# A two-layer attention and expert kernel: the second layer's gate weights are turned on VectorE instead of TensorE

## What is computed

```python
logits = jnp.dot(x, Wr) + br                                  # 32 per token
aff = jax.nn.sigmoid(logits)
top_v, top_i = jax.lax.top_k(aff, 8)
top_w = top_v / (jnp.sum(top_v, axis=-1, keepdims=True) + 1e-09)
w_full = zeros((T, 32)).at[arange(T)[:, None], top_i].set(top_w)
shared = dot(silu(dot(x, Wg_s) + bg_s) * (dot(x, Wu_s) + bu_s), Wd_s) + bd_s
gate = silu(einsum('th,ehi->eti', x, Wg) + bg)
up = einsum('th,ehi->eti', x, Wu) + bu
down = einsum('eti,eih->eth', gate * up, Wd) + bd
routed = einsum('te,eth->th', w_full, down)
```

## Time and profile before

| | |
|---|---|
| three runs | 491.8, 491.97 and 492.65 us, median 491.97 |
| profiled execution | 493.67 us |
| its span, first to last instruction | 491.9 us |
| instructions | 8510 |
| mean granted TensorE clock | 0.99 of full |
| TensorE / VectorE / ScalarE / GpSimd busy | 455.2 / 398.6 / 281.6 / 269.6 us |
| the 16 transposes of `weights1` on TensorE, one | 273 ns |
| the 4 copies to `hs` on ScalarE, one | 585 ns |
| store of 64 KB to `wt_dram`, issue to landing | 1.6 us median, 3.4 us at most |

### The profile page before, as it was taken

The page is one execution under the profiler, slowest core; times in us unless marked ns, Lnnn a source line. Parts: engine busy times, 40 slices in busy tenths (PEclk is TensorE's granted clock), DMA queues, the critical chain, the costliest instruction groups (busy, mean ns, idle before and its releaser), DMA issues.

```text
span 491.9 us, 8510 instructions
## 1 busy us (share of the span) xinstructions
PE 455.2 (93%) x3072; PEld 219.5 (45%) x3072; DVE 398.6 (81%) x812; ACT 281.6 (57%) x456; POOL 269.6 (55%) x237
## 2 busy tenths in 40 slices
PE   2999888889999999999999999999889998989995
PEld 2755447434444345453454444544334453423332
DVE  1634457999998988899999978978999999986785
ACT  2264673446767635738876445556776537467640
POOL 6322360235554775547763459636675865546982
PEclk9999997999999999999999999999999999999998
DMA  7900059786952710232569643025592662204201
GB/s 277 338 14 0 22 182 194 127 142 182 234 111 76 127 18 4 73 84 65 176 181 168 111 62 91 1 65 171 178 172 43 121 98 77 58 5 113 59 2 43
DMA packets 54754, 52.44 MB, mean 107 GB/s; under 512 B 5080, under 2 KB 44344, under 8 KB 54072
## 3 DMA queue, kind: packets, MB, share of 16 engines
q1 hardware_dynamic: 54712, 51.90, 44.2%
HBM read 37.47 MB, written 13.89 MB: 104 GB/s over the span
## 4 chain that ended last, share of the span: by engine, by line
PE 73%; DVE 18%; ACT 3%; issue 2%; POOLq 1%; DMA 1%; POOL 1%; SPq 0%; DVEq 0%; ACTq 0%
PE bank L785 10%; PE bank L776 9%; PE bank L797 8%; PE scores L816 8%; PE bank L871 5%; DVE nmax L1335 3%; PE scores L711 3%; PE scores L702 3%; PE scores L726 3%; PE scores L705 3%; PE scores L810 3%; PE scores L750 3%; DVE h L1311 3%; PE bank L876 2%; DVE h L1318 2%
## 5 line engine op out<-in xcount | busy, mean ns | idle before, releaser
L1136 POOL TENSOR_TENSOR gb<-gb,wb 128x512 f32<-128x512 f32 x64 | 84.3, 1318 | 94.3 <-ACT gb L1024 76.3
L1039 ACT ACTIVATE pk<-scores 128x1024 f32<-128x1024 f32 x96 | 95.3, 1023 | 38.9 <-PE scores L816 38.7
L1129 POOL TENSOR_SCALAR_AFFINE_SELECT pk<-pk 128x512 f32<-128x512 f32 (+1 forms) x96 | 82.1, 864 | 39.8 <-ACT pk L1039 39.3
L1335 DVE TENSOR_REDUCE nmax<-scores 128x8 f32<-128x1024 f32 x64 | 76.4, 1216 | 7.7 <-PE scores L816 7.0
L1021 ACT ACTIVATE gt<-bank,bgh 128x512 f32<-128x512 f32 (+1 forms) x68 | 46.7, 687 | 62.5 <-PE bank L776 50.7
L785 PE MATMUL bank<-xnt,wu 128*128 128x512 f32 x128 | 68.3, 615 | 2.3 <-DVE h L1318 2.2
L776 PE MATMUL bank<-xnt,wg 128*128 128x512 f32 x128 | 69.4, 624 | 0.0
L797 PE MATMUL bank<-h,wd 128*128 128x512 f32 x128 | 66.5, 617 | 0.0
L1311 DVE SCALAR_TENSOR_TENSOR h<-gt,gb 128x512 f32<-128x512 f32 x64 | 57.8, 903 | 3.4 <-PE bank L797 3.1
L1318 DVE SCALAR_TENSOR_TENSOR h<-bank,bu,h 128x512 f32<-128x512 f32 x64 | 48.1, 751 | 10.8 <-PE bank L785 8.8
L1140 POOL TENSOR_TENSOR orms<-oms,minus_half 128x32 f32<-128x32 f32 x8 | 44.7, 5585 | 10.3 <-DVE oms L1365 10.3
(11 more groups left out here) (262 smaller groups left out, 711.1 us busy)
## 6 DMA issues: line engine op xcount, KB each, us to landing
wb<-wt_scratch SPq DMA_DIRECT2D x64, 256.0 KB, 4.2
parts_scratch<-parts SPq DMA_DIRECT2D x16, 384.0 KB, 3.0
qa<-parts_scratch SPq DMA_DIRECT2D x32, 192.0 KB, 4.9
ka<-parts_scratch SPq DMA_DIRECT2D x32, 192.0 KB, 5.9
parts_scratch<-parts SPq DMA_DIRECT2D x16, 256.0 KB, 3.1
parts_scratch<-parts SPq DMA_DIRECT2D x16, 128.0 KB, 2.8
ha<-in_wkq SPq DMA_DIRECT2D x1, 1024.0 KB, 4.8
wb<-in_wvo SPq DMA_DIRECT2D x1, 1024.0 KB, 7.5
```

Of the source, the lines that this page charges most:

```text
L1039: A(dst.rearrange("p (h m) q -> p m h q", m=2), pairs[pair_of(step)][:, :, :].rearrange("p m (h q) -> p m h q", q=cols), ACT.Exp, scale=SC ...
L1129: pool.affine_select(out=dst, in_=dst, compare_op=ALU.is_ge, fill=0.0, base=0, pattern=[[0, heads], [1, P]], channel_multiplier=-1).then_i ...
L1136: pw(gb[:, c % 2, :], gb[:, c % 2, :], wb[:, k % 2, j % 2, :], ALU.mult).then_inc(s_ga_done, 1)
L1335: V.tensor_reduce(dst, src, AX, ALU.max, negate=True).then_inc(s_nmax_done, 1)
```

## The change

The four transposes and the copy of `weights1` are gone from TensorE and ScalarE, and `weights1` from the orders `FRONT` and `BANK4`. Instead `choose1` ends on VectorE with one more instruction: a transpose of `wtok`, taken as 128 x 128, into the new `wturn`. VectorE's transpose works in blocks of 32 by 32, so `wturn` holds, in partition 32 g + e and column 32 k + j, the weight of expert e for token 128 k + 32 g + j. Before it stands a wait for the store of the chunk before. The step `weights1` of SyncE now waits for `s_w_done` and stores `wturn` to the same place in `wt_dram`, with an address pattern that puts each run of 32 tokens where it belongs. The 32 rows of `hs` for the shared expert are loaded back from `wt_dram` by SyncE in the step `wb/8c`, before the two transfers of `wb`; for chunks 2 and 3 this first waits until `down` of the chunk two before is done. `down` of the shared expert waits for that load, `s_wt_in`.

```diff
--- before.py
+++ after.py
@@ -69,11 +69,10 @@
 
 
 FRONT = ("load", "norm0", "scale0", "turn0", "keys0", "router0", "inner0", "scores0", "picks0", "probs0", "hidden0",
-         "hidden1", "out0", "back0", "norm1", "scale1", "turn1", "router1", "choose1", "queries1", "keys1", "store", "values1",
-         "weights1")
+         "hidden1", "out0", "back0", "norm1", "scale1", "turn1", "router1", "choose1", "queries1", "keys1", "store", "values1")
 RING = ("turn0", "keys0", "inner0", "scores0", "picks0", "probs0", "hidden0", "hidden1", "out0", "turn1", "router1",
         "queries1", "keys1", "values1", "max", "score", "fin")
-BANK4 = ("minus", "values", "weights1", "out1")
+BANK4 = ("minus", "values", "out1")
 
 
 def order(text):
@@ -239,6 +238,7 @@
         rest1 = sb("rest1", [P, TILES, E1])
         wsum = sb("wsum", [P, TILES])
         wtok = sb("wtok", [P, TILES, E1])
+        wturn = sb("wturn", [P, TILES * E1])
         hs = sb("hs", [INNER + E1, 2, CHUNK])
         wb = sb("wb", [P, 2, 2, CHUNK])
         qkf = sb("qkf", [P, 4, CHUNK])
@@ -365,8 +365,7 @@
         s_rl_done = sem("rl_done")
         s_rexp_done = sem("rexp_done")
         s_w_done = sem("w_done")
-        s_wt_ps = sem("wt_ps")
-        s_wt_sb = sem("wt_sb")
+        s_wt_in = sem("wt_in")
         s_wt_stored = sem("wt_stored")
         s_wb_in0 = sem("wb_in0")
         s_wb_in1 = sem("wb_in1")
@@ -423,7 +422,7 @@
                    s0_ps=CB, nb0=1, p0_done=TILES, pt_ps=CB, pt_sb=CB, att_ps=1, logits_ps=1, u_ps=1, lsub=1,
                    lexp_done=1, um_done=2, umt_ps=2, umt_sb=2, inter_ps=FB, inter2_ps=FB, ha_done=FB, hb_done=FB,
                    hsum_done=FB, zt_ps=1, zt_sb=1, z_ps=1, z_read=1, th0_done=TILES, var1=1, rstd1=1, xn1_done=TILES, xnt1_ps=1,
-                   xnt1_sb=1, router_ps=1, rl_done=1, rexp_done=1, w_done=1, wt_ps=1, wt_sb=1, wt_stored=16,
+                   xnt1_sb=1, router_ps=1, rl_done=1, rexp_done=1, w_done=1, wt_in=16, wt_stored=16,
                    qk_ps=4, qk_rest=4, part1=4, part2=4, part3=4, parts_stored=16 * 6, v_ps=2, v_sb=2,
                    max_ps=CB * UNITS, nmax_done=CB * UNITS, mp_done=CB, mrow_ps=CB, mrow_sb=CB, mrow_in=CB * MROWS_IN,
                    sc_ps=CB * UNITS, pk_done=CB * UNITS, pk_masked=CB * UNITS, pv_ps=CB * GROUPS, 
@@ -507,8 +506,6 @@
                 pe.wait_ge(s_mrow_sb, at(c, "mrow_sb", rest[0] + 1))
             elif kind == "values":
                 pe.wait_ge(s_oc_done, group(c, *rest) + 1)
-            elif kind == "weights1":
-                pe.wait_ge(s_wt_sb, at(c, "wt_sb", 1))
             elif kind == "out1":
                 pe.wait_ge(s_s1_read, at(c, "s1_read", 1))
 
@@ -560,12 +557,18 @@
                                          mrows[m * 3 * HEADS:(m + 1) * 3 * HEADS, b * SEQ:(b + 1) * SEQ]).then_inc(s_mrow_in, 16)
                     elif kind == "weights1":
 
-                        sp.wait_ge(s_wt_sb, at(c, "wt_sb", 1))
-                        sp.dma_start(t["wt_dram"][c], hs[INNER:INNER + E1, c % 2, :]).then_inc(s_wt_stored, 16)
+                        sp.wait_ge(s_w_done, at(c, "w_done", 1))
+                        dst = t["wt_dram"][c].rearrange("e (k g j) -> g e k j", g=P // QUAD, j=QUAD)
+                        sp.dma_start(dst, wturn[:, :]).then_inc(s_wt_stored, 16)
                     elif kind == "wb":
 
                         k, slot = c % (PAIRS // 2), c % 2
                         sp.wait_ge(s_wt_stored, at(c // (PAIRS // 2), "wt_stored", 16))
+                        if k == 0:
+                            n = c // (PAIRS // 2)
+                            if n >= 2:
+                                sp.wait_ge(s_acc_ps, (n - 1) * STEPS)
+                            sp.dma_start(hs[INNER:INNER + E1, n % 2, :], t["wt_dram"][n]).then_inc(s_wt_in, 16)
                         if c >= 2:
                             sp.wait_ge(s_ga_done, 2 * (c - 1))
                         src = t["wt_dram"][c // (PAIRS // 2)].rearrange("(j e) t -> e j t", e=2)
@@ -755,12 +758,6 @@
                                   start=(k % 2 == 0), stop=True, skip_group_check=True)
                         if k % 2:
                             last.then_inc(s_v_ps, 1)
-                elif name == "weights1":
-
-                    pe.wait_ge(s_w_done, at(c, "w_done", 1))
-                    for k in range(TILES):
-                        last = nc.tensor.transpose(bank[4][0:E1, k * P:(k + 1) * P], wtok[:, k, :], ident[:, :])
-                    last.then_inc(s_wt_ps, 1)
 
             def gate(n):
                 c, j = divmod(n, STEPS)
@@ -791,7 +788,7 @@
                     if c:
                         pe.wait_ge(s_fg_done, at(c - 1, "fg_done", 1))
                 if j == PAIRS:
-                    pe.wait_ge(s_wt_sb, at(c, "wt_sb", 1))
+                    pe.wait_ge(s_wt_in, at(c, "wt_in", 16))
                     m = mm(bank[7], wds[:, :], hs[:, c % 2, :], start=False, stop=True)
                 else:
                     m = mm(bank[7], wd[:, j, :], h1[:, n % HR, :], start=(j == 0), stop=False)
@@ -993,13 +990,6 @@
                         act.wait_ge(s_v_ps, at(c, "v_ps", n + 1))
                         A(v1[:, 2 * n:2 * n + 2, :, 0:DV].rearrange("p c h d -> p (c h) d"),
                           pairs[pair][:, n, :].rearrange("p (g d) -> p g d", d=DV), ACT.Copy).then_inc(s_v_sb, 1)
-                elif name == "weights1":
-                    if c >= 2:
-
-                        act.wait_ge(s_acc_ps, (c - 1) * STEPS)
-                        act.wait_ge(s_wt_stored, at(c - 2, "wt_stored", 16))
-                    act.wait_ge(s_wt_ps, at(c, "wt_ps", 1))
-                    A(hs[INNER:INNER + E1, c % 2, :], bank[4][0:E1, :], ACT.Copy).then_inc(s_wt_sb, 1)
 
             for step in PROGRAM:
                 kind, c, *rest = step
@@ -1288,7 +1278,10 @@
 
                     link(V.tensor_scalar(wsum[:, :], wsum[:, :], 1e-9, 2.0, ALU.add, ALU.mult))
                     link(V.reciprocal(wsum[:, :], wsum[:, :]))
-                    V.tensor_tensor(wtok[:, :, :], wtok[:, :, :], wide(wsum[:, :], E1), ALU.mult).then_inc(s_w_done, 1)
+                    link(V.tensor_tensor(wtok[:, :, :], wtok[:, :, :], wide(wsum[:, :], E1), ALU.mult))
+                    if c:
+                        dve.wait_ge(s_wt_stored, at(c - 1, "wt_stored", 16))
+                    V.transpose(wturn[:, :], wtok[:, :, :].rearrange("p k e -> p (k e)")).then_inc(s_w_done, 1)
                 elif name in ("queries1", "keys1"):
                     first = 0 if name == "queries1" else 2
                     for f in range(2):
```

## The result

| | before | after |
|---|---|---|
| median of 15 executions each, side by side | 492.78 us | 495.39 us |
| ratio, after to before | | 1.0061, 95% interval 1.0040 to 1.0083 |
| profiled execution | 493.67 us, span 491.9, mean granted clock 0.990 | 493.63 us, span 491.9, mean granted clock 0.987 |

The changed kernel is slower by 2.6 us in the medians; I had forecast 1.4 us less, and the result lies above my range as well. The difference is small against the spread of single executions (after: 493.54 to 500.51), and the two profiled executions last equally long. So the profiles can't be compared by their ends, but they can by their stages: I take the start of the same TensorE step (such as the first matmul of `gate/22`) in both and follow how the difference of the two starts changes.

A forecast was written before the change was run, and what follows sets the result against it. TensorE was taken as the bound (93% busy, 73% of the chain). Chunk terms 0, -0.54 + 0.16, -0.54 and -0.65 + 0.16 sum to -1.41 us against the 491.97 median: 490.6 us, 8-in-10 range 489.4 to 493.1.

The forecast's parts named there:

- VectorE's transpose, 0.31 us.: End of each `choose1`: the added 128x128 transpose takes 0.31 us, 0.33 us per chunk with its link.
- Chunk 0, store and `wb/0`.: Chunk 0: the store lands at about 89.5 and `wb/0` arrives when it did, worth 0.
- The rival of the slow store: Chunk 0: 128-byte packets at 130 ns bring `wb/0` 2.7 us later, ending at 493.2 us; chance 0.16.
- Chunk 0, "the transposes are worth 0": Chunk 0: removing TensorE's transposes gains 0, since VectorE's queue is full until 96.91 and covers them.
- Chunk 1, -0.54 + 0.16.: Chunk 1: removed TensorE transposes give -0.54 us; VectorE's added transpose, partly absorbed in standing behind GpSimd, costs +0.16.
- Chunk 2, "`choose1` isn't on the chain. 0": Chunk 2: VectorE's added transpose costs 0, since the chain is on TensorE when `choose1` ends.
- 0.33 if it were: Chunk 2: bound on the added transpose's cost if `choose1` were on the chain, 0.33 us.
- The term for the removal, -0.54: Chunk 2: taking TensorE's transposes off the chain at 250.74 gives -0.54 us.
- Chunk 3, -0.65 + 0.16.: Chunk 3: removed transposes and ScalarE copy give -0.65 us near 386; VectorE's added transpose near 357 costs +0.16.
- The rival "not passed on": Chunks 1 to 3: transposes unabsorbed, half the 1.73 us gain given back; about +0.15, stated as 491.7 us; chance 0.27.

The follow-up runs named there:

- the run with the old chunk 2: New way in chunk 0 alone, chunks 1 to 3 as in the kernel before: 492.92 us, ratio 0.9995 to before.
- the pairs: Two kernel pairs differing in chunk 0's way: new in chunks 0-3 against 1-3 (495.19, 494.82 us); 0-2 against 1-2, chunk 2's transpose late (494.61, 492.59 us).
- the late transpose: Kernel before with new way in chunks 1 and 2, chunk 2's VectorE transpose moved behind `minus/2/0`: 493.07 us, then 492.59 us; ratio 0.9996 both times.

## Why the prediction was wrong

- **VectorE's transpose, 0.31 us.** Right: 0.312, so the figure that the Trainium skill ("VectorE: DVE Perf Modes", "The three transpose paths") gives for bf16, 311 ns, holds for these 4-byte numbers too.
- **Chunk 0, store and `wb/0`.** Right on both: landed when forecast, GpSimd's multiply unmoved. The price that I gave to small pieces was near: 47 ns for each of the 24 packets more that an engine has would make 1.1 us, and in chunk 1, where it can be compared, they add 1.44 us. The Trainium skill ("DMA: Bandwidth & Descriptors", "Specifications") says that transfers under 512 B are read, modified and written; the trace agrees in so far as they cost more. The rival of the slow store, which had the right sign and nearly the right time (493.2), is wrong in its mechanism.
- **Chunk 0, "the transposes are worth 0".** Wrong in a way for which I had no term. They held no place in the chain and cost no time in before, but they kept TensorE at work; without them the mean granted clock is lower by 0.004 to 0.006, which is 1.2 to 1.7 us at 0.29 us for each 0.001. I had counted an idle engine as free.
- **Chunk 1, -0.54 + 0.16.** The transpose: absorbed wholly, 0 instead of 0.16, and by the mechanism that I gave: the product behind it takes 1.05 us where it took 1.39 (in chunk 3 0.80 instead of 1.15), since GpSimd holds its time. (The product ends 0.56 us after GpSimd's multiply, not 0.68 as I read it; nothing hangs on it.) The removal: -0.28 instead of -0.54. What follows on TensorE starts 0.44 us earlier, not 0.54, and its first matmul takes 0.70 us instead of 0.59; no new wait stands there. The sign was right; off by 0.10 in sum.
- **Chunk 2, "`choose1` isn't on the chain. 0".** This is the first step that failed, and it failed by 1.17 us. My bound "0.33 if it were" was wrong too: a delay of 0.33 us can turn the order of two engines' instructions, and what follows then isn't 0.33 but a product of 1.50 instead of 0.68 us. I had seen this standing behind GpSimd in the earlier trace rows, and used it only as cover in which a delay disappears. The term for the removal, -0.54, looks right and isn't: without VectorE's transpose chunk 2 gains 0.50, but only 0.21 of it by `gate/26`, and 0.29 at the step behind it, where the run with the old chunk 2 has them as well. That the two add up to nearly 0.54 is luck. With VectorE's transpose in place TensorE's are worth nothing: from `gate/25` to `gate/26` the kernel loses 0.97 us with them and without them.
- **Chunk 3, -0.65 + 0.16.** The second step that failed, by 1.5 us. The transpose at 356 costs 0, and the chain from 386 on is shorter as I said, but the time gained puts ScalarE's `gb`, and with it GpSimd's multiply, ahead of the product, twice. Of the 0.56 us gained by 391.5 (forecast 0.65) all is lost and 1.0 more. The term for it would have been: what does an earlier ScalarE trigger, and what stands 0.17 us away from it (in before, 393.80 and 393.97).
- **The rival "not passed on"** had half of the mechanism (freed time is given back at the next wait), but ended at 491.7, or -0.3 (its own sum, +0.15, would be 492.1), because I let it take no more than what had been gained.

The sum as it turned out: 0 - 0.28 + 0.67 + 1.00 = +1.4 us from the stages, +2.4 to +2.7 measured. That leaves 1.0 to 1.3 us for the granted clock, where its mean, lower by 0.0053 over after's 33 executions, would make 1.5. The first part is shown stage by stage; the second rests on means of executions, and the pairs give 0.7 and 1.6 for it, while chunk 0's new way alone, against before, shows nothing in its ratio (0.9995).

No version beats the kernel before by more than the runs can tell. The stages say that chunks 1 and 2 in the new way with the late transpose gain 0.65 us (0.13%); measured are 0.9996 twice, and 1.0004 for the one with chunk 0 in the new way and its TensorE transposes kept.

## What to carry to other kernels

Where VectorE's products of two tensors and GpSimd's instructions run side by side, write down how far apart they start, and ask of each edit whether it turns one of these orders; in this kernel a turned order made a product longer by 0.8 to 1.0 us each time, nearly three times the edit's own length, whether the edit made something later or earlier. Work that is off the chain on TensorE isn't worthless: taken out of chunk 0, where TensorE often waits, it made low clock more frequent. And an effect of half a per cent is found by comparing starts of the same steps stage by stage, since single executions of one and the same kernel differ by more.

## What was unexpected of the hardware

- The same product (128x512, two inputs in SBUF, one output) takes 0.68 us when it starts 0.01 us before GpSimd's multiply and 1.55 us when it starts 0.28 us behind; GpSimd's multiply takes 1.81 us in the first case and 1.27 in the second. In these rows whoever comes second takes longer. The Trainium skill ("SBUF — State Buffer", "Who interferes with whom") says this as a rule: a VectorE instruction with two SBUF inputs contends with a GpSimd instruction that reads SBUF, as an exclusive lock, and the order of issue decides. The rows agree, for GpSimd's masks as well (1.50 against 0.68).
- VectorE's transpose took 312 ns for 128x128 numbers of 4 bytes, in all four chunks, near other work or not.
- A store of 64 KB took 1.44 us longer in pieces of 128 bytes than in pieces of 512 (3.19 against 1.75).
- Executions with a mean granted clock at or under 0.984 were 15 of 148 in before, 4 of 35 with chunk 0 in the new way and TensorE's transposes kept, and 30 of 81 without these four transposes, which take 0.6 us together.
- The exponential behind one and the same score unit of chunk 2 starts 0.28 us sooner behind its matmuls (idle 0.79 instead of 1.07 us) in the run that leaves a copy of 0.58 us out of ScalarE's work two chunks earlier and nothing out of chunk 2. No row says why.
